# Stage 7's expert outputs, added to two per-token sums in DRAM by accumulating transfers instead of scattered as four rows a token

## The reference

```python
def _L3_ffn_ref(x, router_w, router_bias, gate_w, up_w, down_w, sgate_w, sup_w, sdown_w):
    flat = x.reshape(B * T, D)                                   # 2048 x 256
    scores = softmax(flat @ router_w.T + router_bias)            # 32 experts
    topk_scores, topk_idx = jax.lax.top_k(scores, 4)
    topk_scores = topk_scores / topk_scores.sum(axis=-1, keepdims=True)
    h = silu(einsum('nd,ehd->neh', flat, gate_w)) * einsum('nd,ehd->neh', flat, up_w)
    expert_out = einsum('neh,edh->ned', h, down_w)
    sel = take_along_axis(expert_out, topk_idx[:, :, None], axis=1)
    out = (sel * topk_scores[:, :, None]).sum(axis=1)
    return out + silu(flat @ sgate_w.T) * (flat @ sup_w.T) @ sdown_w.T
...
x = x + tanh(g_ffn[3]) * _L3_ffn_ref(_layernorm(x), ...)
```

## Time and profile before

| what | value |
|---|---|
| median of 3 runs | 1433.05 us (1427.53 to 1437.87) |
| the profiled execution, span from first to last instruction | 1420.1 us |
| PE busy | 1224.4 us, 86% of the span |
| DVE busy | 719.4 us, 51% |
| POOL busy | 293.1 us, 21% |
| DMA | 186.75 MB, mean 131 GB/s |

### The profile page before, as it was taken

How to read it: one execution, slowest core, us unless ns; L and a number is a source line. 1 busy time by engine, 2 the same in 40 slices (tenths; PEclk the granted TensorE clock), 3 DMA queues, 4 the chain that set the end, 5 groups by cost and what they waited for, 6 DMA issues and landing times.

```text
span 1420.1 us, 19370 instructions
## 1 busy us (share of the span) xinstructions
PE 1224.4 (86%) x6360; PEld 763.7 (54%) x6361; DVE 719.4 (51%) x2069; ACT 443.1 (31%) x826; POOL 293.1 (21%) x347
## 2 busy tenths in 40 slices
PE   5999999999876998999988769999567698999984
PEld 3634434434432444443443649999556456887762
DVE  7264474478965346545752531111376742455457
ACT  2132232233533445444434103333242211333320
POOL 2111111130021001001000041111113662355560
PEclk9899999999977999999998679999876799999997
DMA  9999999000000000000100845555229223454437
GB/s 313 338 336 335 332 327 298 23 8 1 1 0 1 1 0 1 2 0 1 33 1 1 258 134 202 177 176 181 103 84 318 91 91 111 123 151 150 145 109 303
DMA packets 140425, 186.75 MB, mean 131 GB/s; under 512 B 8673, under 2 KB 124897, under 8 KB 140225
## 3 DMA queue, kind: packets, MB, share of 16 engines
q1 hardware_dynamic: 130800, 159.28, 36.3%
q0 software_dynamic: 9552, 26.52, 5.1%
HBM read 83.71 MB, written 102.06 MB: 131 GB/s over the span
## 4 chain that ended last, share of the span: by engine, by line
PE 67%; DVE 14%; issue 8%; ACT 4%; DMA 3%; SPq 3%; POOL 0%; another core or an unknown queue 0%; DVEq 0%; POOLq 0%; ACTq 0%
PE psum L1960 13%; PE psum L1248 6%; PE psum L1259 6%; PE psum L2171 5%; PE psum L2228 3%; DVE arena L2764 2%; PE psum L920 2%; PE psum L2252 2%; PE psum L2205 2%; PE psum L2153 2%; PE psum L1953 2%; PE psum L1988 2%; PE psum L1917 2%; PE psum L931 2%; PE psum L1058 1%
## 5 line engine op out<-in xcount | busy, mean ns | idle before, releaser
L1960 PE MATMUL psum<-arena 128*128 128x512 f32 x432 | 196.9, 604 | 0.0
L2764 DVE TENSOR_REDUCE arena<-psum 128x4 f32<-128x616 f32 x128 | 102.1, 798 | 114.7 <-PE psum L2171 113.4
L1960 PEld LDWEIGHTS psum<-arena 128*128 128x128 f32 x432 | 79.7, 191 | 112.8 <-issue 111.8
L2171 PE MATMUL psum<-arena 32*128 32x308 f32 x512 | 109.6, 506 | 25.6 <-DVE arena L2764 24.3
L1166 POOL DMA_INDIRECT ys<-xnT,arena x96 | 92.1, 959 | 109.0 <-DVE xnT L1143 86.5
L2352 ACT ACTIVATE arena<-psum,arena 128x512 f32<-128x512 f32 x72 | 49.0, 685 | 164.6 <-PE psum L1960 154.9
L2443 ACT ACTIVATE arena<-psum 128x2048 f32<-128x2048 f32 x40 | 75.0, 1874 | 62.8 <-PE psum L2209 45.8
L2171 PEld LDWEIGHTS psum<-arena 32*128 32x128 f32 x512 | 42.1, 198 | 92.9 <-DVE arena L2764 59.6
L1039 PE MATMUL psum<-arena,xn 128*128 x384 | 87.1, 380 | 2.3 <-ACT xn L1089 1.9
L1248 PEld LDWEIGHTS psum<-side,arena 128*128 128x128 f32 x736 | 87.4, 195 | 2.7 <-ACT side L1293 1.6
L1248 PE MATMUL psum<-side,arena 128*128 128x128 f32 x736 | 87.9, 279 | 1.0 <-ACT side L1293 1.0
(11 more groups left out here) (402 smaller groups left out, 2083.9 us busy)
## 6 DMA issues: line engine op xcount, KB each, us to landing
xs<-zeros SPq DMA_DIRECT2D x8, 8576.0 KB, 59.3
arena<-in_W SPq DMA_DIRECT2D x31, 1024.0 KB, 12.0
xn<-xs SPq DMA_DIRECT2D x64, 134.0 KB
arena<-in_gate_up SPq DMA_DIRECT2D x4, 2048.0 KB, 16.2
arena<-ys SPq DMA_DIRECT2D x4, 2048.0 KB, 14.8
arena<-xs SPq DMA_DIRECT2D x32, 134.0 KB
arena<-in_down SPq DMA_DIRECT2D x4, 1024.0 KB, 15.5
xs<-zeros SPq DMA_DIRECT2D x1, 2990.0 KB, 16.0
```

The lines of the kernel that those rows point to most:

```text
L1960: ins = pe.matmul(bank[dict(hn=4, r=5, z=6, xn=7)[k]][:], lhs[:, cols], r, start=(start and n == 0), stop=(stop and n == len(w) - 1))
L2171: ins = pe.matmul(bank[4 + i][:, 0:2 * M].rearrange("p (h m) -> p h m", h=2), qhT[rows, n % 3, c, t * P:(t + 1) * P], keys[rows, l, c, b, ...
L2764: dve.tensor_reduce(neg[:, n % 2, t, 2 * pair:2 * pair + 2, 2 * c:2 * c + 2], psum[:, 4:6, 0:2 * M].rearrange("p b (h m) -> p b h m", h=2) ...
```

## The change

Instead of four rows a token in ys7 there are two tensors sums7_0 and sums7_1 in DRAM, each with one row a token and 256 rows behind them. The four row numbers of a token are all the same, 1 + token (the iota has a step of 0 over k), and rows without a token go to 128 spare rows. POOL's scatters carry compute_op=add: the transfer adds the rows from SBUF to those in DRAM. Tiles t = 0 and 2 of a quad go to sum 0, t = 1 and 3 to sum 1. As a token may have rows in two tiles in a row, every scatter waits until the one before on the same sum has landed (semaphores added7_0, added7_1). A tile belongs to one expert, so that no token is in it twice. DVE's copy_out of quad q waits on both semaphores until all of quad q-2 has landed, which is the same condition as before. Both sums are filled with zeros at the start, between the fills of xs5 and xs7. The end reads two rows a token (eight transfers of 512 KB), and DVE adds them in two passes a group.

```diff
-        gathered7 = arena[:, GU0:GU0 + T * K4 * D].rearrange("p (t k d) -> p t k d", t=T, k=K4)
+        sums7_in = arena[:, GU0:GU0 + 2 * T * D].rearrange("p (a t d) -> p a t d", a=2, t=T)
...
-        ZEROINGS = 1 + (SPARE + 1 + 63) // 64
+        ZEROINGS = 3 + (SPARE + 1 + 63) // 64
...
-        ys7 = nc.dram_tensor("ys7", (1 + T * P * K4 + NT4 * P, D), F32, kind="Internal").ap()
+        sums7 = [nc.dram_tensor(f"sums7_{a}", ((T + 2) * P, D), F32, kind="Internal").ap() for a in range(2)]
...
-            for u in range(2):
-                sp.wait_ge(*sent[u].at(7, NQ // 2 * 64))
+            for a in range(2):
+                sp.wait_ge(added7[a], 16 * 2 * NQ)
             for g in range(G):
-                sp.dma_start(gathered7[:, g * GT:(g + 1) * GT],
-                             ys7[1 + g * GN * K4:1 + (g + 1) * GN * K4].rearrange("(t p k) d -> p t k d", p=P, k=K4)
-                             ).then_inc(gathered_in[g].sem, 16)
+                for a in range(2):
+                    sp.dma_start(sums7_in[:, a, g * GT:(g + 1) * GT],
+                                 sums7[a][1 + g * GN:1 + (g + 1) * GN].rearrange("(t p) d -> p t d", p=P)
+                                 ).then_inc(gathered_in[g].sem, 16)
...
-                    dve.wait_ge(*sent[q % 2].at(7, 64 * (q // 2)))
+                    for a in range(2):
+                        dve.wait_ge(added7[a], 16 * 2 * (q - 1))
...
                 for t in range(4):
-                    pool.indirect_dma_start(ys7, bass.IndirectOffsetOnAxis(row_i[:, u, t:t + 1].bitcast(U32), 0),
-                                            qout[:, u, t * D:(t + 1) * D], None).then_inc(sent[u].sem, 16)
+                    a, earlier = t % 2, 2 * q + t // 2
+                    if earlier:
+                        pool.wait_ge(added7[a], 16 * earlier)
+                    pool.indirect_dma_start(sums7[a], bass.IndirectOffsetOnAxis(row_i[:, u, t:t + 1].bitcast(U32), 0),
+                                            qout[:, u, t * D:(t + 1) * D], None, compute_op=ALU.add).then_inc(added7[a], 16)
...
-            for k in range(K4):
-                ins = dve.tensor_tensor(xs, xs, gathered7[:, g * GT:(g + 1) * GT, k], ALU.add)
-                if k < K4 - 1:
-                    ch.step(ins)
-                    ch.settle()
-            ins.then_inc(x_done.of(7), 1)
+            ch.step(dve.tensor_tensor(xs, xs, sums7_in[:, 0, g * GT:(g + 1) * GT], ALU.add))
+            ch.settle()
+            dve.tensor_tensor(xs, xs, sums7_in[:, 1, g * GT:(g + 1) * GT], ALU.add).then_inc(x_done.of(7), 1)
...
+                for a in range(2):
+                    sp.dma_start(sums7[a].rearrange("(t p) d -> p t d", p=P),
+                                 zeros[:, 0:D].unsqueeze(1).broadcast_to([P, T + 2, D])).then_inc(zeroed, 16)
...
-                pool.iota(xn[:].rearrange("p g t d -> p (g t) d")[:, :, D + 2 * K4:], [[K4 * P, T], [1, K4]], base=1,
-                          channel_multiplier=K4, allow_small_or_imprecise_dtypes=True).then_inc(rowid_made, 1)
+                pool.iota(xn[:].rearrange("p g t d -> p (g t) d")[:, :, D + 2 * K4:], [[P, T], [0, K4]], base=1,
+                          channel_multiplier=1, allow_small_or_imprecise_dtypes=True).then_inc(rowid_made, 1)
...
-                pool.iota(unused_row, [[P, NT4]], base=1 + T * P * K4, channel_multiplier=1,
+                pool.iota(unused_row, [[0, NT4]], base=1 + T * P, channel_multiplier=1,
                           allow_small_or_imprecise_dtypes=True).then_inc(rowid_made, 1)
```

More of the change, by code:

```diff
@@ L528, in build @@
         extras5_ready, rowid5_made = (sem(k) for k in ("extras5_ready", "rowid5_made"))
-        gathered_in = [series(f"gathered_in{g}", {s: 16 for s in (5, 7)}) for g in range(G)]
+        gathered_in = [series(f"gathered_in{g}", {5: 16, 7: 32}) for g in range(G)]
+        added7 = [sem(f"added7_{a}") for a in range(2)]
         (shares_shifted, shares_exp, shared_hid, shared_done, shared_added, shared_down, shared_tanh, qtanh_ready,
@@ L536, in build @@
         wr7_loaded = sem("wr7_loaded")
-        sent = [series(f"sent{u}", {5: 16 * ((NT2 + 1 - u) // 2), 7: 16 * 4 * NQ // 2}) for u in range(2)]
+        sent = [series(f"sent{u}", {5: 16 * ((NT2 + 1 - u) // 2)}) for u in range(2)]
         w6_loaded, max_found, max_turned, max_diag, max_spread, w6_rounded, kp_done, kp_ready, ctx6_done, ctx6_ready = (
@@ L1165, in scatter_out_gpsimd @@
                 for t in range(4):
-                    pool.indirect_dma_start(ys7, bass.IndirectOffsetOnAxis(row_i[:, u, t:t + 1].bitcast(U32), 0),
-                                            qout[:, u, t * D:(t + 1) * D], None).then_inc(sent[u].sem, 16)
+                    a, earlier = t % 2, 2 * q + t // 2
[3 more added lines that the diff above has]
+                                            qout[:, u, t * D:(t + 1) * D], None, compute_op=ALU.add).then_inc(added7[a], 16)
         def combine7_vector(dve, ch, g):
             dve.wait_ge(shared_added, 2 * (g + 1))
-            dve.wait_ge(*gathered_in[g].at(7, 16))
+            dve.wait_ge(*gathered_in[g].at(7, 32))
             ch.settle()
             xs = x_tok[:, g * GT:(g + 1) * GT]
-            for k in range(K4):
-                ins = dve.tensor_tensor(xs, xs, gathered7[:, g * GT:(g + 1) * GT, k], ALU.add)
-                if k < K4 - 1:
-                    ch.step(ins)
-                    ch.settle()
-            ins.then_inc(x_done.of(7), 1)
+            ch.step(dve.tensor_tensor(xs, xs, sums7_in[:, 0, g * GT:(g + 1) * GT], ALU.add))
+            ch.settle()
+            dve.tensor_tensor(xs, xs, sums7_in[:, 1, g * GT:(g + 1) * GT], ALU.add).then_inc(x_done.of(7), 1)
         def last_group_vector(dve, ch):
```

## The result

The changed kernel takes 1471.08 us (median of 4 runs, 1464.71 to 1473.83) against 1430.29 us for the kernel before beside it (4 runs, 1424.14 to 1437.87): a ratio of 1.0268, 95% interval 1.0217 to 1.0319. It is slower by 2.7%. The profiled execution has a span of 1462.9 us and its own time is 1464.71.

The account below looks back on a forecast made before the run. PE was taken to pace the quads (7.28 us each), with DMA engines full at the end. Span 1420.1 - 6.3 for the shorter end with chains + 1 for contention = 1415, plus 12.95 carried over: 1428 us, range 1422 to 1490.

Parts of the forecast that it names:

- the chain sets the pace: Rival, POOL's scatters on one sum: L above 3.64, span 1221.3 + 48L + 19, gain gone at L = 3.75; chance 0.34.
- L: Time from one scatter's issue to the next issue that waits for it; taken as 3.5 us, hidden in steady quads below 3.64.
- step (b): Scatters in the quads become two serial chains; L = 2.70 plain + 0.36 second read + 0.44 fixed = 3.5 us.
- T + 19: Predicted end of the span, in us, T being when the last scatter has landed; last group at T + 13.4.
- The 12.95 us carried over: Median of the runs (1433.05) less the profiled span before (1420.1), added unchanged to the predicted span.
- (a): The end reads half the bytes and does half the passes; PE's shared expert sets a floor of 1411.5, worth at most 8.6 us.
- (c): Contention in the quads: 4 x 128 KB more each delays the next quads' loads; taken as 1 us.
- (d): Two more zero fills at the start: 14 us on SP until 253, 34 us of cover remain, so no cost.
- (e): Iotas write as many columns; at the end SP issues eight reads for four, 0.5 us each, hidden behind the first reads' bytes.
- Transfers of 6 us under load: Rival, scatters in the quads: transfers under load take about 6 us, span 1528, +108; L above 5.5 had chance 0.12.
- The accumulate at a plain scatter's cost: Rival, scatters in the quads: L up to about 3.2, end at PE's floor 1411.5, median 1424.5; chance 0.12.
- The signs named for "wrong": In the quads: POOL waits for its own DMA, DVE for sums before copy-out, PE's busy share under 91%, clock below 1.00.

Follow-up runs that it names:

- e9: The kernel before, repeated without an edit: ratio 1.0025 to before, first scatter at 1230.94, 195.2 us from there to the end.
- e11: A second unedited copy of the kernel before: ratio 1.0007 to before, first scatter at 1231.03, 199.2 us from there to the end.
- e4: The kernel before, its end reading and adding only two of each token's four rows: 1414.55 us, ratio 0.9914 to before.
- e1: The changed kernel without compute_op, so plain overwriting scatters with the same serial waits: 1415.48 us, ratio 0.9913 to before.
- e6: The changed kernel with scatters of 128 columns for 256, fills and reads of half the size: 1447.65 us, ratio 1.0210 to before.
- e5: The changed kernel with POOL's two waits before a quad's first scatter in the other order: ratio 1.0330 to before, 231.3 us from the first scatter.
- e7: The changed kernel with the quads' loads fetching only the last columns, 4% of the bytes: 1458.69 us, ratio 1.0299 to before.
- e3: The kernel before with two more zero fills at the start, into tensors that nothing reads: ratio 1.0017 to before.
- e2: The changed kernel with four sums in place of two, each scatter waiting only for the quad before: 1445.30 us, ratio 1.0103 to before.
- e8: The kernel before with the changed kernel's serial waits, plain scatters still to four rows a token: 1424.12 us, ratio 1.0056 to before.

## Why the prediction was wrong

The forecast was 1428 us, within 1% of before; the measured 1471.08 is slower, inside the range of 1422 to 1490, in the case that had 0.34: the chain sets the pace. The structure held and one term was mis-sized: L, in step (b), 3.5 us in the forecast and 4.52 in the trace. With L = 4.52 in the rival's formula, 1240.3 + 48 x 4.52 = 1457.3 us; the quads began 4.1 us later than in the profile of before, less than the same code varies by (e9, e11), and the end took 2 us more than T + 19: together 1463.4, for a measured 1462.9. That so much agrees by L alone is the formula's merit; the range held only because it took in the rival's case.

The 12.95 us carried over are mostly something else than the text ahead of the prediction says. What lies ahead of the first and behind the last instruction is 1.8 us in the changed kernel's profiled execution (1464.71 - 1462.9). The rest is that the profile of before is of a short execution: its quads begin at 1220.01, those of e9 and e11, the same kernel, at 1230.94 and 1231.03.

**(a) The shorter end** was right in kind. It is worth 11.0 us (e4), not 8.6. The floor of PE's last matmuls moved with the clock, since they took 7.15 us where I had carried over 8.83. In the changed kernel two things make T + 21.1 out of T + 19. The read is slower than the 384 GB/s that I used: its second group landed in time for DVE at 1451.02, 1.3 us later than 1441.8 + 5.5 + 2.4, and the last part at about 1456.8, at T + 15.1 and not T + 13.4. And from 1451.02 on DVE never idles: two passes, the last shared part and four passes until 1459.60 are 8.6 us in a row, which the sum, with only the last two passes behind the last landing, had left out. By my own rate DVE would have ended 0.9 us after the sum's time (an estimate: 1449.7 + 8.6 + 3.3 against T + 19). "No slower than the above" was the wrong reading of rows 7: those rows bounded one landing, not a rate.

**(b) L, the step that failed.** I had it as 2.70 + 0.36 + 0.44 = 3.5. The base holds only as the least: e1 shows 2.67 at least, but 3.20 in the mean where a plain scatter in a quad was released by a landing. What was measured, each in its own place:

| part | predicted | difference measured | where |
|---|---|---|---|
| POOL's issue | not counted | +0.59 (1.55 for 0.96) | the groups of after and e1 |
| time of the engines for the transfer | +0.36 | +0.78 (1.12 for 0.34) | the queue's rows, e6 |
| a second wait at a quad's border | not counted | +0.22 (0.44 every second time) | e5, and the chain |
| loads beside it | in (c) | +0.18 | e7 |
| share of a load's fixed time | +0.44 | not seen apart | no run isolates it |

The sum is 2.70 + 0.59 + 0.78 + 0.22 + 0.18 = 4.47, which is close to 4.52, but that isn't proof: only the waits' order (e5), the loads (e7) and the bytes (e6) were changed by themselves, and the table puts the least value of a plain transfer under the mean of an accumulating one. Like for like, within a quad and released by a landing, the accumulate adds 1.25 us at the least (3.92 for 2.67) and 0.93 in the mean (4.13 for 3.20), where the table has 0.59 + 0.78 = 1.37. So it is shown that the accumulate adds about 1 us to each step of the chain, and that its issue (0.59 us more on POOL) and its time on the engines (0.78 more) are both longer; how they share that 1 us, and whether a fixed part as I had guessed is in it, stays open. The 0.36 priced the bytes of the second source and took the packets as they were; in fact they went from 48 to 143 a scatter of 128 rows. And I costed what the transfer does but not what its issue does on POOL: "POOL must build descriptors for a second source" stood in the rival and had no number. With 0.59 alone added, L = 4.09 would have been past the break-even of 3.75.

By the Trainium skill, DMA: Bandwidth & Descriptors (Anatomy of one DMA), a transfer from GpSimd takes about 2.0 us plus the bytes over 436 GB/s, an estimate of 2.3 us here. For the accumulate the chain shows 3.67 to 4.37 us from issue to landing between 1250 and 1300 us, so the measurement decides: that figure doesn't carry over to this kind.

**(c) Contention** was right in that it is small, wrong in its place: the loads lengthen the chain (0.18 x 48 = 8.6 us, e7), where I had 1 us for loads that come later. As long as PE had been the bound, 1 us might have done; with the transfers as the bound, each delay counted in full.

**(d) The fills and (e) the issues** show no cost, as said: SP's first load of the attention weights was issued at 252.75 (predicted 253), and e3 shows no loss. SP's eight reads take 7.58 us to issue, where 0.5 us each would be 4: one of them takes 2.61. They lie beside the transfers; whether that one holds up the last group is not shown.

**The rivals.** Transfers of 6 us under load didn't come (e7: the load's share is small). The accumulate at a plain scatter's cost is what e1 shows of plain transfers, and it gives 0.9913, which is the gain of the shorter end alone (e4, 0.9914): so all of the loss, and more, is in the accumulate. The signs named for "wrong" all came: POOL waits for its own transfers, DVE waits some 5 us (60.5 / 12) for them before its copy-out, PE's busy share fell from 91% to 85% from 1215 to 1371 us (to 82% in the steady part), and the clock to 0.96 (0.94). The prediction's signs sufficed to read L, and L to read the time.

The 42.8 us between the two profiled spans are then accounted for: from the first scatter to the read back 217.7 us (1441.78 - 1224.08) where it was 167.55, that is +50.15; the end gives back 11.4; the start is 4.1 later, by chance.

## What to carry to other kernels

Before independent transfers are turned into a chain, multiply the whole distance from issue to dependent issue (the issue on its engine, the transfer, the step after each wait) by the chain's length, and price each part for the new kind of transfer: here 0.25 us in L stood between my value and the break-even. An accumulating scatter traded fewer bytes at the end for more time on POOL and many more packets in the middle; here POOL did not have the time to issue them even with the chains out of the way (7.44 us a quad in e2 for 7.01 before). And look at the order of two waits before one issue: with the one that is satisfied last put first, each step across quads was 0.38 us shorter here (e5).

## What the runs showed of the hardware that was not expected

- An accumulating indirect scatter of 128 rows of 1 KB takes 1.55 us to issue on POOL (plain 0.96), also with rows of 512 bytes (e6); it has 143 packets (plain 48) and keeps 16 engines busy for 1.12 us (plain 0.34), or 0.70 us with half rows. From issue to landing it takes 3.9 us in the median (e5), with half rows 3.4 (e6), plain 2.6 (e8).
- Where POOL has two waits in front of such an issue and the second is the one that ends last, the step from landing to issue is 0.71 to 0.73 us for 0.27 in the chain; with the order turned it is 0.27, and the distance across quads 0.38 us less (e5).
- With the engines full, the read in runs of 1 KB moves 346 GB/s (changed kernel, 1444 to 1457 us), in runs of 2 KB, two rows of a token beside each other, 389 (e4, 1392 to 1404), in runs of 4 KB 414 (before, 1392 to 1404), stores of x_tok included.
- The same code is granted a clock of 1.00 in one execution and 0.93 in another in the same stretch of the start, and all that follows moves by up to 11 us, 0.8% of the span. In this kernel a profile's absolute times late in the span aren't comparable to better than that; distances from a common event are.
